# One attention bias in two made by ScalarE in the first turn, and the branch on the mask flag moved from mid-kernel to the end of the setup

## Chip, cores, metric

One NeuronCore of a Trainium2 chip runs the whole program. The metric is device time in microseconds of one execution, as the median of the runs. The kernel is written by hand, engine by engine, with semaphores: TensorE (PE, with its weight loads shown apart as PEld), VectorE (DVE), ScalarE (ACT), GpSimd (POOL), and SyncE (SP), which issues nearly all DMAs.

## What is computed

Two transformer layers over x of shape 8 x 512 x 256 with 16 heads of width 16. The first layer adds to the scores a bias that depends on the pair of positions and, by a factor, on the head:

```
# layer 0
h = layer_norm(x) * g + b, modulated by gelu(time_emb) @ Wt + bt
scores = q @ k.T / 4 - torus_dist[None] * torus_scale[head]
scores = where(pad, -1e30, scores)          # mask_BxS_bf1
x = x + softmax(scores) @ v @ Wout;  x = x + gelu(layer_norm(x) @ W1 + b1) @ W2 + b2
# layer 1: no such bias; keys masked by mask_BxS_bk0
ada = silu(c @ ada1) @ ada2 -> shifts, scales, gates of both branches
x = x + gate * modulate(norm(attention(x))); x = x + gate * modulate(norm(mlp(x)))
```

## The kernel before

The program is a setup ("prologue"), then N = 16 **turns**, then an epilogue. Turns 0 to 7 are layer 0 for the eight sequences (B = 8), turns 8 to 15 are layer 1. Each engine has its own program and its own `prologue`, `turn(n)` and `epilogue`; `run` strings them together. A turn also carries dense work of its neighbours (the table FIRST says which piece goes into which step): turn n does projections for sequence n+1 and the MLP of n-1, so turn 0 has less matmul work than turns 1 to 7, since nothing comes before it.

A turn of layer 0 has 32 **units** (a head and half of the queries each) of two 128x512 score tiles. In step k, PE does `scores(k)` (two matmuls, each into its own PSUM bank, so tile t waits until DVE has read tile t-2), every fourth step (k = 7, 11, ..., 31) `attend` (32 small matmuls), then `turn_unit(k-2)` (eight transposes), every fourth step (k = 9, 13, ...) `to_tokens`, and the dense pieces. DVE's `shift_scores(u)` (L1406) adds the bias to the scores, writes `shifted` and the row maximum; POOL's `subtract_max(u)` (L633, two instructions) follows; PE transposes the result; ACT's `exps(u)` (L1117, two instructions) takes the exponential.

The bias of a unit, 128x1024 elements, is one multiplication of `dist` by the head's `scale`. In the kernel before it is made by POOL (L626) for three units in four and by ACT (L1106) for the units with u % 4 == 3. There are two bias buffers, so that `make_bias(u)` waits for the shift of unit u-2. Both engines are in-order: POOL makes the bias of unit k+2 behind `subtract_max(k)`, and ACT makes it behind `exps(k-1)`, that is `exps(u-3)`, and ahead of `take_out` (L1125) and the dense pieces of its step k+1. DVE's wait counts the biases made so far, on one semaphore for each maker.

Layer 1 exists in two versions: a short one, for when no key is masked outside the last 128, and a general one. DVE computes a flag from the masks in its prologue (L1493 to L1499); SP stores it to DRAM (L481), in the kernel before behind the first two groups of q and k rows and the modulation rows. Before turn 8 each of the five engines waits for the store, loads the flag into a register and branches to one of two copies of turns 8 to 15. Here the short version is taken.

SP's prologue, after the loads: it stores two quarters of the q and k rows of sequence 0 (`store_half`, L373), loads the first group back in the layout that PE needs (`load_group(0, 0)`, L397 to L409), stores the other quarters, loads the second group, stores `mod_rows` and the flag, and copies rows of ones. PE's first scores wait for the first group.

DVE's prologue ends with the modulation rows (L1503 to L1510) and the low halves of `w_out` and `w_up` (L1226).

Of the kernel before, what the change touches and what calls it, by code (L numbers as in the profile page):

```python
# [18 lines left out]
def build(nc, d, out):  # L19
    B, L, D = d["x"].shape  # L20
# [15 lines left out]
    UNITS = 2 * H  # L36
# [11 lines left out]
    N = 2 * B  # L48
# [53 lines left out]
    def amid(n, k):  # L102
        return n > 0 and k in AMID

    def bias_by_act(u):
        return u % 4 == 3

    def pass_of(piece, n):
        m = n - 1 if piece[0] in BACK else n + 1 if piece[0] in FRONT else n
# [21 lines left out]
    with ExitStack() as ctx:  # L131
# [6 lines left out]
        def sem(name):  # L138
            return ctx.enter_context(nc.semaphore(name))
# [8 lines left out]
        flags = dram("flags", (1, 1), I32)  # L148
# [86 lines left out]
        early_flag = sb("early_flag", [1, 1], I32)  # L235
# [29 lines left out]
        s = {name: sem(name) for name in names}  # L265
# [51 lines left out]

        def run(eng, prologue, turn, epilogue):
            prologue()
            for n in range(B):  # L320
                turn(n)
            eng.wait_ge(s["flag_stored"], 16)
            flag = eng.value_load(flags[0:1, 0:1], min_val=0, max_val=1)
            with eng.If(flag > 0):
                chosen["any"] = 1
                for n in range(B, N):
                    turn(n)
                epilogue()
                chosen["any"] = 0
            with eng.Else():  # L330
                for n in range(B, N):
                    turn(n)
                epilogue()

# [3 lines left out]
        def _(sp):  # L338
# [106 lines left out]
            def prologue():  # L445
                with nc.allow_non_contiguous_dma(reason="small vectors laid on partitions"):
                    load_x(0)
                    load_mask(0)
                    load(cond_t[:, 0, :], d["cond_1024"][:, 0:P].rearrange("b p -> p b"), "cond_loaded")
                    load(cond_t[:, 1, :], d["cond_1024"][:, P:D].rearrange("b p -> p b"), "cond_loaded")  # L450
                    load(w_t, d["L0_cond_Wt"].rearrange("(c p) n -> p c n", p=P), "cond_loaded")
                    load(bt_col[:, :], d["L0_cond_bt"].rearrange("(c p) -> p c", p=P), "cond_loaded")
                    load(ln1_gb[:, 0, :], d["L0_cond_ln1_g"].rearrange("(c p) -> p c", p=P), "cond_loaded")
                    load(ln1_gb[:, 1, :], d["L0_cond_ln1_b"].rearrange("(c p) -> p c", p=P), "cond_loaded")
                    load(raw_qkv, d["L0_cond_Wqkv"].rearrange("(c p) n -> p c n", p=P), "wqkv_loaded")
                    load(scale[:, :], d["L0_cond_torus_scale"].unsqueeze(0).broadcast_to([P, H]), "dist_loaded")
                    load(dist[:, :, :], d["L0_cond_torus_dist"][0].rearrange("(t p) k -> p t k", p=P), "dist_loaded")
                    load(ada1, d["L1_cond_ada1_w"].rearrange("(c p) n -> p c n", p=P), "ada_loaded")
                    load(ada1_col[:, :], d["L1_cond_ada1_b"].rearrange("(c p) -> p c", p=P), "ada_loaded")
                    load(ada2, d["L1_cond_ada2_w"].rearrange("(c p) n -> p c n", p=P), "ada_loaded")  # L460
                    load(ada, d["L1_cond_ada2_b"].unsqueeze(0).broadcast_to([B, 6 * D]), "ada_loaded")
                    load(all_masks[:, :], d["mask_BxS_bk0"][:, 0:EARLY], "masks_loaded")
                    load(ln2_gb[:, 0, :], d["L0_cond_ln2_g"].rearrange("(c p) -> p c", p=P), "rest_loaded")
                    load(ln2_gb[:, 1, :], d["L0_cond_ln2_b"].rearrange("(c p) -> p c", p=P), "rest_loaded")
                    load(out_bias[:, :], d["L1_cond_proj_b"].unsqueeze(0).broadcast_to([P, D]), "rest_loaded")
                    load(raw_out[0], d["L0_cond_Wout"].rearrange("(c p) n -> p c n", p=P), "wout_loaded")
                    load(raw_up[0], d["L0_cond_W1"].rearrange("(c p) n -> p c n", p=P), "wup_loaded")
                    load_down("L0_cond_", "W2", "b1", "b2")
                x_free(0)
                load_x(1)  # L470
                store_half(0, 0)
                store_half(0, 1)
                sp.wait_ge(s["ones_set"], 2)
                load_group(0, 0)
                store_half(0, 2)
                store_half(0, 3)
                load_group(0, 1)
                sp.wait_ge(s["mod_ready"], 1)
                sp.dma_start(mod_rows, mod_out).then_inc(s["mod_stored"], 16)
                sp.wait_ge(s["flag_ready"], 1)  # L480
                sp.dma_start(flags, early_flag[:, :]).then_inc(s["flag_stored"], 16)  # L481
                for a in range(2):
                    for x in range(2):
                        at = PEAK_AT + 2 * a + x
                        sp.dma_start(k_rows[at:at + 1, :, :, a, :].bitcast(F32),
                                     q_rows[MASK_AT:KROWS, 0:2, :, :].bitcast(F32)).then_inc(s["row_ones"], 16)
# [115 lines left out]
        def _(pool):  # L602
# [127 lines left out]
            def turn(n):  # L730
                if short(n):
                    short_turn(n)
                    return
                if n < B:
                    make_bias(n, 0)
                    make_bias(n, 1)
                    if 0 < n < B - 1:
                        inverse_std(n + 1, 0)
                    for k in range(UNITS):
                        subtract_max(n, k)  # L740
                        if k + 2 < UNITS and not bias_by_act(k + 2):
                            make_bias(n, k + 2)
                        if k == 4 and n == 0:
                            inverse_std(1, 0)
                        if k == 11 and n > 0:
                            inverse_std(n - 1, 1)
                        if k in ADD_BIAS and n > 0:
                            add_bias(n - 1, ADD_BIAS[k])
                        if k == 18:
                            pool.wait_ge(s["bias_ready"], 24 * n + k + 3 - (k + 3) // 4)  # L750
                            mask(n + 1)
                    if n + 1 == B:
                        value_mask(B)
                    return
                back(n - 1)
                if n + 1 < N:
                    mask(n + 1)
                    value_mask(n + 1)
                if n > B:
                    inverse_std(n - 1, 1)  # L760
# [290 lines left out]
        def _(act):  # L1051
# [120 lines left out]
            def turn(n):  # L1172
                if short(n):
                    for p in range(HEAD_STEPS):
                        for k in range(3 * p, 3 * p + 2):
                            for piece, m in pieces(HEADS, k, n):
                                dense(piece, m)
                        if p == 0 and n - 2 >= B:
                            normalize(n - 2)
                        if 6 <= p < 6 + 2 * G and p % 2 == 0:  # L1180
                            take_heads_out(n, (p - 6) // 2)
                        if 4 <= p < 4 + H // 2:
                            for a in range(2):
                                head_exp(n, 2 * (p - 4) + a)
                        if 2 <= p < 2 + H // 2:
                            load_peaks(n, p - 2)
                        for piece, m in pieces(HEADS, 3 * p + 2, n):
                            dense(piece, m)
                        if n == B and p == 6:
                            take_high(w_out, raw_out[1], "wout_loaded", "out_high", 2)  # L1190
                        if n == B and p == HEAD_STEPS - 1:
                            take_high(w_up, raw_up[1], "wup_loaded", "up_high", 2)
                    return
                for k in range(STEPS):
                    if k >= OUT and (k - OUT) % 4 == 0:
                        take_out(n, (k - OUT) // 4)
# [1 line left out]
                        dense(piece, m)  # L1198
                    if 1 <= k <= UNITS:
                        exps(n, k - 1)  # L1200
                    if n < B and k + 2 < UNITS and bias_by_act(k + 2):
                        make_bias(n, k + 2)
                    if n == B - 1 and k in (6, 7):
                        take_qkv_high(k - 6)
# [18 lines left out]
        def _(dve):  # L1223
# [172 lines left out]
            def shift_scores(n, u):  # L1396
                for i in range(2):
                    t = 2 * u + i
                    if n < B and i == 0:
                        if bias_by_act(u):  # L1400
                            dve.wait_ge(s["act_bias_ready"], 8 * n + u // 4 + 1)
                        else:
                            dve.wait_ge(s["bias_ready"], 24 * n + u + 1 - (u + 1) // 4)
                    dve.wait_ge(s["scores_ready"], TILES * n + t + 1)
                    if n < B:
                        dve.tensor_tensor_reduce(shifted[:, u % 3, i, :], score_bank[t % 2], bias[:, u % 2, i, :],  # L1406
# [220 lines left out]
```

## Time and profile before

| | us |
|---|---|
| median of 3 runs (1373.4, 1373.43, 1377.46) | 1373.43 |
| the profiled execution's own time | 1377.58 |
| its span, first to last instruction | 1375.7 |

| engine | busy, us | share of the span |
|---|---|---|
| PE | 1287.0 | 94% |
| DVE | 796.0 | 58% |
| POOL | 754.5 | 55% |
| ACT | 744.4 | 54% |

The first scores of turn 0 start 44.42 us into the span, its last transposes run at about 125 us, and the branch lies between 855 and 860 us. The profile gives for each instruction its start and duration and, for an engine that sat idle before it, how long and what released it. Unit u of turn 0 is the u-th pair of L1406 instructions from 45.38 us on.

### The profile page before, as it was taken

The numbers are of one execution on the slowest core, as the hardware profiler recorded it, in microseconds if no ns is written. First come the engines' busy times: TensorE is split into PE (matmuls) and PEld (weight loads), VectorE is DVE, ScalarE is ACT, GpSimd is POOL, SyncE is SP. The second block draws the span as 40 slices with busy tenths as digits, with TensorE's granted clock in tenths as the row PEclk, the third lists the DMA queues.
The fourth block names the chain that finished last, engine by engine and source line by source line (L and its number), as shares of the span: only waits on it lengthen the run. The fifth ranks groups of instructions, "written<-read, shape, count | busy, mean of one in ns | idle before, by whom it ended". The sixth has DMA issues, their size and how long they took to land. (4 is left out here: it accounts for less than half of the span.)

```text
span 1375.7 us, 24533 instructions
## 1 busy us (share of the span) xinstructions
PE 1287.0 (94%) x8789; PEld 995.1 (72%) x8789; DVE 796.0 (58%) x2240; ACT 744.4 (54%) x1246; POOL 754.5 (55%) x939
## 2 busy tenths in 40 slices
PE   4799999999999999999999998899999999999878
PEld 3567778778778778778778776767677676766656
DVE  3766845845845845845844843556656566564552
ACT  3466674674674674674674673454444444444431
POOL 3688876876876876866866864101224032240323
PEclk9899999999999999999999999899999999999888
DMA  8533231331331331331331340726243352434100
GB/s 257 145 96 91 63 116 41 77 116 39 79 116 37 80 117 35 81 117 33 80 121 30 94 132 28 225 72 201 76 155 126 115 169 77 154 108 118 47 2 31
DMA packets 98259, 133.98 MB, mean 97 GB/s; under 512 B 16802, under 2 KB 51498, under 8 KB 98130
## 3 DMA queue, kind: packets, MB, share of 16 engines
q1 hardware_dynamic: 96850, 131.80, 32.5%
q8 instruction: 73, 1.20, 0.4%
q10 hardware_dynamic: 1280, 0.53, 0.2%
q14 instruction: 56, 0.46, 0.1%
HBM read 72.64 MB, written 58.75 MB: 96 GB/s over the span
## 5 line engine op out<-in xcount | busy, mean ns | idle before, releaser
L1406 DVE CUSTOM_DVE_ANT_0 shifted<-score,bias 128x512 f32<-128x512 f32 x512 | 332.1, 686 | 281.1 <-PE score L873 202.5
L633 POOL TENSOR_SCALAR shifted<-shifted,row_max 128x512 f32<-128x512 f32 x512 | 362.3, 720 | 171.3 <-DVE row_max L1406 168.4
L1117 ACT ACTIVATE probs<-turned 128x512 f32<-128x512 f32 x512 | 277.6, 595 | 218.8 <-PE turned L885 218.6
L885 PE MATMUL turned<-ident,shifted 128*128 128x128 f32 x2048 | 269.6, 274 | 4.4 <-ACT probs L1117 4.3
L885 PEld LDWEIGHTS turned<-ident,shifted 128*128 128x128 f32 x2048 | 232.8, 141 | 56.3 <-issue 32.7
L801 PE MATMUL dense<-w_down,hidden 128*128 128x256 f32 x1024 | 261.8, 382 | 2.4 <-ACT hidden L1098 2.4
L626 POOL TENSOR_SCALAR bias<-dist,scale 128x1024 f32<-128x1024 f32 x192 | 214.5, 1118 | 13.5 <-DMA down_bias<-in_L_cond_b 13.5
L873 PE MATMUL score<-k_rows,q_rows 97*128 97x512 f32 x512 | 202.2, 456 | 14.1 <-DMA k_rows<-mask_neg 5.2
L801 PEld LDWEIGHTS dense<-w_down,hidden 128*128 128x128 f32 x1024 | 178.1, 190 | 36.9 <-issue 9.6
L781 PE MATMUL dense<-feat_m,w_up 128*128 128x512 f32 x768 | 192.9, 403 | 9.4 <-DVE feat_m L1363 9.4
L781 PEld LDWEIGHTS dense<-feat_m,w_up 128*128 128x128 f32 x768 | 144.5, 193 | 42.4 <-issue 11.7
L873 PEld LDWEIGHTS score<-k_rows,q_rows 97*128 97x128 f32 x512 | 92.5, 191 | 48.3 <-DVE row_max L1406 32.4
L1098 ACT ACTIVATE hidden<-dense,up_bias 128x512 f32<-128x512 f32 x128 | 87.3, 688 | 73.9 <-PE dense L781 73.6
L900 PE MATMUL pv<-probs,v_ext 128*32 128x256 f32 x2048 | 123.8, 382 | 0.2 <-DVE attn L1431 0.2
L647 POOL CAST mask_colf<-mask_col 128x4 f32<-128x4 uint8 x8 | 1.5, 186 | 188.9 <-PE pv L952 181.2
L781 PE MATMUL dense<-feat_a,w_qkv 128*128 128x512 f32 x384 | 102.3, 410 | 2.8 <-DVE feat_a L1360 2.8
L1133 ACT ACTIVATE probs<-turned 128x512 f32<-128x512 f32 x128 | 69.4, 596 | 57.4 <-PE turned L942 57.3
L900 PEld LDWEIGHTS pv<-probs,v_ext 128*32 128x32 f32 x2048 | 60.2, 109 | 53.6 <-issue 14.3
L1440 DVE TENSOR_REDUCE row_max<-score 128x8 f32<-128x1024 f32 x64 | 78.4, 1225 | 35.1 <-PE score L923 34.0
L781 PEld LDWEIGHTS dense<-feat_a,w_qkv 128*128 128x128 f32 x384 | 70.6, 194 | 16.5 <-issue 3.2
L1085 ACT ACTIVATE qk_high<-dense 128x512 fp32r<-128x512 f32 x64 | 38.2, 598 | 74.2 <-PE dense L781 55.2
L1106 ACT ACTIVATE bias<-dist,scale 128x1024 f32<-128x1024 f32 x64 | 73.7, 1151 | 0.0
(138 smaller groups left out, 1472.0 us busy)
## 6 DMA issues: line engine op xcount, KB each, us to landing
qk_rows<-qk_high SPq DMA_DIRECT2D x128, 256.0 KB
q_rows<-qk_rows SPq DMA_DIRECT2D x64, 384.0 KB
qk_rows<-qk_low SPq DMA_DIRECT2D x64, 256.0 KB
k_rows<-qk_rows SPq DMA_DIRECT2D x68, 192.0 KB
x_in_t<-in_x SPq DMA_DIRECT2D x8, 512.0 KB, 4.8
x_res<-in_x SPq DMA_DIRECT2D x8, 512.0 KB, 5.6
x_mid<-x_norm SPq DMA_DIRECT2D x8, 512.0 KB, 3.3
x_in_t<-x_mid SPq DMA_DIRECT2D x8, 512.0 KB, 4.1
```

Of the source, the lines that this page charges most:

```text
L626: pool.tensor_scalar(bias[:, u % 2, :, :], dist[:, 2 * half:2 * half + 2, :], scale[:, h:h + 1], 0.0, ALU.mult, ALU.add).then_inc(s["bias_ ...
L633: ins = pool.tensor_scalar(shifted[:, u % 3, i, :], shifted[:, u % 3, i, :], -1.0, row_max[:, t % 6:t % 6 + 1], ALU.mult, ALU.add)
L781: mm = pe.matmul(out_ap, left, right, start=(i == 0), stop=(i == len(terms) - 1))
L801: mm = pe.matmul(bank_of(piece, m)[:, 0:D], hidden[:, c, P * i:P * i + P], w_down[:, c, :], start=(c == 0), stop=(c == FCH - 1))
L873: pe.matmul(score_bank[t % 2], q_rows[0:KROWS, g % 2, j // 2, q0:q0 + P], k_rows[0:KROWS, g % 2, j // 2, j % 2, :], start=True, stop=True) ...
L885: mm = pe.transpose(turned_bank[z % 2][:, HALF * kk + P * i:HALF * kk + P * i + P], shifted[:, u % 3, i, P * kt:P * kt + P], ident[:, :])
L900: mm = pe.matmul(pv_bank[SLOT * j:SLOT * j + SLOT, 0:HALF], v_ext[:, kt, HG * (gq // 2) + j, :], probs[:, (4 * gq + j) % RING, kt, :], sta ...
L1098: act.activation(hidden[:, i, :], bank[:, :], ACT.Gelu_apprx_tanh if m < B else ACT.Gelu, bias=up_bias[:, i:i + 1]).then_inc(used(piece, m ...
L1106: act.activation(bias[:, u % 2, :, :], dist[:, 2 * half:2 * half + 2, :], ACT.Copy, scale=scale[:, h:h + 1]).then_inc(s["act_bias_ready"], 1)
L1117: act.activation(probs[:, u % RING, 2 * pair:2 * pair + 2, :], turned_bank[z % 2][:, :].rearrange("p (a c) -> p a c", a=2), ACT.Exp)\
L1406: dve.tensor_tensor_reduce(shifted[:, u % 3, i, :], score_bank[t % 2], bias[:, u % 2, i, :], 1.0, 3.0e38, ALU.add, ALU.min, row_max[:, t % ...
L1440: dve.tensor_reduce(row_max[:, :].rearrange("p (a t) -> p t a", a=2), pair_scores, mybir.AxisListType.X, ALU.max).then_inc(s["peak_ready"], 1)
```

## The change

In turn 0 ACT makes the bias of every odd unit; the other turns keep one in four. `make_bias(0, 1)`, which POOL made ahead of the units, goes to the head of ACT's turn. The waits count biases with a function. The flag is stored ahead of the first group of rows, and all engines branch at the end of their prologue, so that all 16 turns stand in both copies.

```diff
-    def bias_by_act(u):
-        return u % 4 == 3
+    def bias_by_act(n, u):
+        return u % 2 == 1 if n == 0 else u % 4 == 3
+    def biases(n, u, act):
+        return sum(bias_by_act(m, v) == act for m in range(n + 1) for v in range(UNITS if m < n else u + 1))
...
         def run(eng, prologue, turn, epilogue):
             prologue()
-            for n in range(B):
-                turn(n)
             eng.wait_ge(s["flag_stored"], 16)
             flag = eng.value_load(flags[0:1, 0:1], min_val=0, max_val=1)
             with eng.If(flag > 0):
                 chosen["any"] = 1
-                for n in range(B, N):
+                for n in range(N):
                     turn(n)
                 epilogue()
                 chosen["any"] = 0
             with eng.Else():
-                for n in range(B, N):
+                for n in range(N):
                     turn(n)
                 epilogue()
...
                 store_half(0, 1)
+                sp.wait_ge(s["flag_ready"], 1)
+                sp.dma_start(flags, early_flag[:, :]).then_inc(s["flag_stored"], 16)
                 sp.wait_ge(s["ones_set"], 2)
                 load_group(0, 0)
...
                 sp.dma_start(mod_rows, mod_out).then_inc(s["mod_stored"], 16)
-                sp.wait_ge(s["flag_ready"], 1)
-                sp.dma_start(flags, early_flag[:, :]).then_inc(s["flag_stored"], 16)
...
                     make_bias(n, 0)
-                    make_bias(n, 1)
+                    if not bias_by_act(n, 1):
+                        make_bias(n, 1)
...
-                        if k + 2 < UNITS and not bias_by_act(k + 2):
+                        if k + 2 < UNITS and not bias_by_act(n, k + 2):
                             make_bias(n, k + 2)
...
+                if n == 0 and bias_by_act(0, 1):
+                    make_bias(0, 1)
                 for k in range(STEPS):
...
-                    if n < B and k + 2 < UNITS and bias_by_act(k + 2):
+                    if n < B and k + 2 < UNITS and bias_by_act(n, k + 2):
                         make_bias(n, k + 2)
...
-                        if bias_by_act(u):
-                            dve.wait_ge(s["act_bias_ready"], 8 * n + u // 4 + 1)
+                        if bias_by_act(n, u):
+                            dve.wait_ge(s["act_bias_ready"], biases(n, u, True))
                         else:
-                            dve.wait_ge(s["bias_ready"], 24 * n + u + 1 - (u + 1) // 4)
+                            dve.wait_ge(s["bias_ready"], biases(n, u, False))
```

## Rows read from the trace of the kernel before

**Rows 1.** The page, busy time by engine.
```profile
PE 1287.0 (94%) x8789; PEld 995.1 (72%) x8789; DVE 796.0 (58%) x2240; ACT 744.4 (54%) x1246; POOL 754.5 (55%) x939
```
**Rows 2.** Busy by window: length, PE, PEld, DVE, ACT, POOL, PEclk, DMA share, GB/s.
```profile
88.00:110.00 22.00, 21.46 (x177) 15.72 (x176) 14.74 (x51) 14.45 (x27) 21.26 (x28) 1.00 0.52 178
...
231.00:331.00 100.00, 98.89 (x782) 78.55 (x781) 59.65 (x184) 64.09 (x108) 77.63 (x97) 1.00 0.29 80
```
**Rows 3.** Waits from 44 to 128 us: total, times, longest.
```profile
DVE shifted L1406 <- ACT bias L1106: 8.5, 7, 2.0
...
DVE shifted L1406 <- POOL bias L626: 2.2, 2, 1.4
```
**Rows 4.** Timeline, units 24 to 27 of turn 0: start, duration, engine, instruction.
```profile
106.32 1.09 ACT L1117 ACTIVATE probs<-turned 128x512 f32<-128x512 f32 x2 [0.38 <-PE turned L885]
...
107.04 0.69 DVE L1406 CUSTOM_DVE_ANT_0 shifted<-score,bias 128x512 f32<-128x512 f32 x1
...
107.86 1.11 POOL L626 TENSOR_SCALAR bias<-dist,scale 128x1024 f32<-128x1024 f32 x1
...
108.35 0.71 PE L873 MATMUL score<-k_rows,q_rows 97*128 97x512 f32 x2
...
109.14 0.68 DVE L1406 CUSTOM_DVE_ANT_0 shifted<-score,bias 128x512 f32<-128x512 f32 x1
...
110.50 1.15 ACT L1106 ACTIVATE bias<-dist,scale 128x1024 f32<-128x1024 f32 x1
...
110.94 1.93 PE L900 MATMUL pv<-probs,v_ext 128*32 128x256 f32 x32
```
**Rows 5.** Timeline, exponentials of unit u-3 and shift of u, u 9 and 13.
```profile
65.45 1.09 ACT L1117 ACTIVATE probs<-turned 128x512 f32<-128x512 f32 x2 [0.94 <-PE turned L885]
...
66.61 0.69 DVE L1406 CUSTOM_DVE_ANT_0 shifted<-score,bias 128x512 f32<-128x512 f32 x1 [0.79 <-POOL bias L626]
...
75.79 1.09 ACT L1117 ACTIVATE probs<-turned 128x512 f32<-128x512 f32 x2 [0.38 <-PE turned L885]
...
77.91 0.69 DVE L1406 CUSTOM_DVE_ANT_0 shifted<-score,bias 128x512 f32<-128x512 f32 x1 [1.49 <-PE score L873]
```
**Rows 6.** Timeline, end of the setup.
```profile
31.29 1.54 SPq L373 DMA_DIRECT2D qk_rows<-qk_high  x1
...
31.77 0.14 DVE L1499 CAST early_flag<-early_any 1x1 int32<-1x1 f32 x1
...
38.84 0.36 SPq L403 DMA_DIRECT2D q_rows<-qk_rows  x1
...
39.21 0.68 DVE L1503 TENSOR_TENSOR shifted<-turned,shifted 8x512 f32<-8x512 f32 x1 [1.04 <-PE turned L985]
...
41.88 2.27 DVE L1226 TENSOR_TENSOR w_up<-probs,w_up 128x2048 fp32r<-128x2048 f32 x1
...
44.42 1.19 PE L873 MATMUL score<-k_rows,q_rows 97*128 97x512 f32 x2 [5.25 <-DMA k_rows<-mask_neg]
...
45.38 0.69 DVE L1406 CUSTOM_DVE_ANT_0 shifted<-score,bias 128x512 f32<-128x512 f32 x1 [1.23 <-PE score L873]
```
**Rows 7.** Timeline around the branch ahead of turn 8.
```profile
854.84 0.38 PE L909 MATMUL pv<-ident,head_out 128*128 128x128 f32 x2
...
859.57 0.62 SPq L409 DMA_DIRECT2D k_rows<-mask_neg  x1
859.68 1.65 PE L781 MATMUL dense<-w_qkv,feat_a 128*128 128x256 f32 x6 [4.46 <-issue]
...
865.26 0.41 SPq L438 DMA_DIRECT2D dist<-in_L_cond_proj_w  x1
...
866.54 0.42 DVE L1376 TENSOR_TENSOR x_res<-x_res,dense 128x256 f32<-128x256 f32 x1 [0.42 <-PE dense L781]
```
**Rows 8.** The load of `x_res` issued at 856.07 us, issue to landing.
```profile
DMA to landing us min/median/max: 6.6/6.6/6.6
```
**Rows 9.** Busy by window behind the branch, columns as in rows 2.
```profile
860.00:862.00 2.00, 2.00 (x11) 2.00 (x11) 0.00 (x0) 0.47 (x1) 0.00 (x0) 0.50 1.10 293
```

More of the change, by code:

```diff
@@ L749, in turn @@
                         if k == 18:
-                            pool.wait_ge(s["bias_ready"], 24 * n + k + 3 - (k + 3) // 4)
+                            pool.wait_ge(s["bias_ready"], biases(n, k + 2, False))
                             mask(n + 1)
```

## The prediction

> **What bounds the kernel now.** I read first the busy times [rows 1]: PE is busy for 94% of the span, the other engines for 54 to 58%, so an edit to ACT or POOL pays only where a stage isn't bound by PE. The windows tell the stages apart [rows 2]. In turns 1 to 7 PE is busy for 98.9 of 100 us. In turn 0, from 88 to 110 us, PE has 21.46 of 22 and POOL 21.26 of 22: both look full, and POOL is the engine that the change relieves. So the question for turn 0 is who waits for POOL. The waits of that turn answer [rows 3]: DVE waited 2.2 us in all for a bias of POOL, twice, and 8.5 us for a bias of ACT, seven times in eight units. POOL is full but in time; the bias that comes late is ACT's, and the change makes more of those.
>
> The timeline shows why [rows 4]. DVE's shift of unit 25 starts at 107.04, right behind unit 24's. PE's scores of unit 26 start at 108.35, DVE's shift of unit 26 at 109.14, ACT's bias of unit 27 runs from 110.50 to 111.65, and DVE waits for it; but in that step PE has `attend`, 1.93 us from 110.94, so the lateness of unit 27 falls under PE's own work. Units with u % 4 == 1 have no `attend` in their step. POOL's bias of unit 26 ends at 107.86 + 1.11 = 108.97, before 109.14: POOL makes it, by 0.17 us.
>
> Setup and branch are read from the timeline too. PE's first scores start at 44.42, released by the DMA of the first group, and DVE's first shift at 45.38 [rows 6]. At the branch PE's last transposes start at 854.84 and end at 855.22, and its next matmul starts at 859.68, after 4.46 us of "issue" idle [rows 7]: nothing but the flag load and the jump. SP, whose instructions are the issues themselves, shows the same price: last issue done at 859.57 + 0.62 = 860.19, next one at 865.26, so **5.07 us** [rows 7].
>
> **Part 1, the branch taken out of the middle.** PE goes straight from 855.22 to turn 8. That would give 4.46 us and more, because in 860 to 862 us the granted clock was 0.50, the lower level of 1.2 GHz, after the 4.46 us of idle [rows 9], and without the idle there is nothing to lower it. What is late next is the load of `x_res`: it lands 6.6 us after its issue at 856.07 [rows 8], at 862.67, and the first `wout` tile's addition, at 866.54 now [rows 7], can't start before 862.7. That is 3.8 us earlier for the first tile. The other `wout` matmuls run meanwhile in the other two banks, and the fourth, which needs the first bank back, then follows at once, so the stream behind comes 3.8 to 4.4 us earlier. I take 4.4, near PE's gap. The ends are 3.8, and 5.7: PE's 4.84 us from issue to issue plus half of the 1.65 us that its first six matmuls took at half the clock [rows 7].
>
> **Part 2, the branch put at the end of the setup.** SP stores the flag right after an issue that ends at 31.29 + 1.54 = 32.83, the flag is ready at 31.91, and SP's next issue waits until 38.84 anyway for the quarters to land [rows 6]: the flag's issue is hidden by that wait, at no cost. I assume it landed by 38.9, with the stores before it. Each engine then pays 5.07 us from where it arrives. ACT and POOL arrive earlier, at 38.9: free at 44.0, and one bias of 1.15 us each is done by 45.2, before DVE's 45.38. PE arrives when DVE's third `ada` addition ends, 39.21 + 0.68 = 39.89: free at 44.96, 0.5 us behind 44.42. SP does its branch before its next wait of turn 0; hidden, unless that slack is gone. DVE is the last: its subtraction for `w_up` starts at 41.88 and ends at 44.15 [rows 6]. Does the flag load wait for its start or its end? PE's row speaks for the start: from 854.84, when the transposes are issued, to 859.68 is 4.84 us, close to SP's 5.07, whereas from their end it is 4.46. I take the start: 41.88 + 5.07 = 46.95 against 45.38, **+1.6 us**; from the end it is 49.22, +3.8. At the low end nothing, if DVE's arrival falls before the flag's landing.
>
> The Trainium skill (Perfetto Trace Analysis, DVE / Act Engine Instruction) says that DVE's sequencer pushes an instruction into a wait queue and is free for the next one while it still waits for its semaphores. By that rule DVE would reach the flag before 41.88 and the sum would be 1.1 to 1.6 us lower. PE's gap doesn't look like that: an engine running ahead of its waits would have loaded the flag while it waited for the `head_out` that released the transposes at 854.84, and no gap would be seen.
>
> **Part 3, eight biases from POOL to ACT.** POOL loses 8 x 1.11 = 8.9 us, which hides behind other work: at most the 2.2 us of [rows 3] are to be had. ACT gains 8 x 1.15 = 9.2 us, each behind the exponentials of unit u-3. For unit 25 those run 106.32 to 107.41 [rows 4]; the bias ends at 108.56, and DVE shifts unit 25 at 108.6 instead of 107.04, 1.55 later. PE's scores of unit 26 need both banks of unit 25: the first is free at about 109.3, the second at 109.95, where now both matmuls run from 108.35 to 109.06. So the transposes, DVE's shift of 26 and `attend` behind them all come about 1.3 us later. PE has nothing else in that step, and the groups follow one another without slack, so this is paid in full. Units 17, 21 and 29 repeat it with 1.1 to 1.3 us. For unit 9 the exponentials end at 66.54 and the bias at 67.69, against a shift at 66.61 [rows 5]: +1.1 for DVE, of which I pass on 1.0. For unit 13 they end at 76.88, the bias at 78.03, against 77.91, with PE busy on `qk`: +0.1. Units 1 and 5 cost nothing: the first is made before the units begin, the second is hidden by the statistics that DVE does ahead of its shift. Sum 1.3 x 2 + 1.2 + 1.1 + 1.0 + 0.1 = **+6.0 us**. Ends: -2.2, if only POOL's waits went, and +9.2, if each bias of ACT were paid in full.
>
> **Sum.** -4.4 + 1.6 + 6.0 = +3.2 us. The profiled execution took 1377.58 us, of which 1375.7 are span; it becomes 1380.8. It lies 4 us over the median of 1373.43, beside the highest of the three runs; the same +3.2 on the median gives **1376.6 us**, 0.23% slower. A measurement of this kernel tells about 0.3%, 4.1 us, from no change, so that my sum stays within it.
>
> **The rivals.**
> - *DVE's branch counts from the end of its last instruction* (slower, over the bound). Place: 44.15 us, DVE. Price 3.8 instead of 1.6: sum +5.4, 1378.8 us. It decides once DVE starts its first shift later than 47.9, where the sum passes 4.1. For it: the flag is loaded with DVE's queue behind a 2.27 us instruction. Against it: PE's 4.84.
> - *POOL is the bound of turn 0* (faster). POOL is full for 21.26 of 22 us [rows 2], and bias 26 is ready with 0.17 us to spare. If the cadence follows POOL, five groups of four units without or with little dense work shrink by one bias, 1.11 each: -5.6 in place of +6.0, sum -8.4, 1365.0 us. Against it: 2.2 us of waits on POOL.
> - *ACT's bias is hidden* (within 0.3%). If PE had slack in those steps, part 3 costs 0 to 2: sum -1.8, 1371.6 us. For it: PE's rows in turn 0 show waits here and there. Against it: the chain in [rows 4].
> - *The change doesn't do what it says*: the flag lands late behind the stores, and all engines branch later. Each microsecond beyond 40.2 is paid once. I count this with the first rival.
>
> **How the numbers follow.** My own sum 0.43, first rival 0.25, POOL 0.13, hidden bias 0.19. Of my own case 0.36 lies within 0.3% and 0.07 above, as parts 1 and 3 each have ends 1 to 3 us off; of the hidden bias 0.14 lies within and 0.05 below. Together: faster 0.18, same 0.50, slower 0.32. The range leaves out the POOL case and a little at the top: 1369.0 covers the hidden bias with a larger gain at the branch, 1381.5 the first rival with part 3 at +8.7.
>
> **What would show it.** Right: the timeline has no gap of PE before turn 8; DVE's first shift at 46.5 to 47.3; waits of DVE on ACT's bias in turn 0 about twice the 8.5 us; turn 0 from first to last shift about 6 us longer. Wrong: a first shift near 49.2 (first rival); groups of turn 0 shorter than now (POOL); waits on ACT doubled, but PE's scores no later (hidden bias); `x_res` not what the first `wout` addition waits for.

## The result, and the profile after

| | before | changed |
|---|---|---|
| median of 14 runs each, us | 1374.33 (1372.57 to 1378.01) | 1380.6 (1376.82 to 1385.64) |
| ratio | | 1.0039, 95% interval 1.0029 to 1.005 |
| profiled execution / its span, us | 1377.58 / 1375.7 | 1382.92 / 1380.7 |

The change makes the kernel 0.39% slower, 5.4 us by the ratio, 5.0 us between the two profiled spans. I had forecast +3.2 us, too little to be told from no change; what came is clear of it. The lines that answer to [rows 6] and [rows 4] are these. First the timeline of the changed kernel (start, duration, engine, instruction, idle before it) around the start of turn 0:

```profile
42.65 2.27 DVE L1232 TENSOR_TENSOR w_up<-probs,w_up 128x2048 fp32r<-128x2048 f32 x1
42.87 3.06 POOL L629 TENSOR_SCALAR bias<-dist,scale 128x1024 f32<-128x1024 f32 x1 [27.55 <-issue]
...
45.54 1.22 PE L877 MATMUL score<-k_rows,q_rows 97*128 97x512 f32 x2 [5.59 <-issue]
...
49.65 0.69 DVE L1412 CUSTOM_DVE_ANT_0 shifted<-score,bias 128x512 f32<-128x512 f32 x1 [4.73 <-issue]
```

PE is at its first scores at 45.54, about where I had put it (44.96), but DVE sits idle for 4.73 us behind its last subtraction and shifts unit 0 at 49.65, not at 46.95. Next units 24 to 28 of turn 0:

```profile
112.55 0.69 DVE L1412 CUSTOM_DVE_ANT_0 shifted<-score,bias 128x512 f32<-128x512 f32 x1 [1.05 <-PE score L877]
...
113.24 1.08 ACT L1121 ACTIVATE probs<-turned 128x512 f32<-128x512 f32 x2 [0.39 <-PE turned L889]
...
114.21 1.15 ACT L1110 ACTIVATE bias<-dist,scale 128x1024 f32<-128x1024 f32 x1
...
115.39 0.69 DVE L1412 CUSTOM_DVE_ANT_0 shifted<-score,bias 128x512 f32<-128x512 f32 x1 [1.54 <-ACT bias L1110]
...
122.25 0.69 DVE L1412 CUSTOM_DVE_ANT_0 shifted<-score,bias 128x512 f32<-128x512 f32 x1 [1.04 <-PE score L877]
```

This is the step that the prediction walked through: exponentials of unit 22, ACT's bias of unit 25 behind them, and DVE waiting 1.54 us for it. From unit 24's shift to unit 25's it is 2.84 us, against 1.41 before (105.63 to 107.04). From unit 24 to unit 28 the four units take 122.25 - 112.55 = 9.70 us; before they took 8.64 (105.63 to 114.27). The waits of this turn, which answer to [rows 3]:

```profile
POOL shifted L636 <- DVE row_max L1412: 22.5, 25, 4.5
...
DVE shifted L1412 <- ACT bias L1110: 18.3, 13, 2.0
```

DVE's wait on ACT's bias went from 8.5 to 18.3 us. POOL, now relieved, waits 25 times for DVE in this turn, where it waited 9 times before. Last, the place where the branch was, which answers to [rows 7] and [rows 9]; in the second fence the columns are those of [rows 2]:

```profile
864.34 0.38 PE L913 MATMUL pv<-ident,head_out 128*128 128x128 f32 x2
864.45 0.77 PEld L785 LDWEIGHTS dense<-w_qkv,feat_a 128*128 128x128 f32 x6
864.47 0.95 PE L785 MATMUL dense<-w_qkv,feat_a 128*128 128x256 f32 x6
...
870.75 1.08 DVE L1382 TENSOR_TENSOR x_res<-x_res,dense 128x256 f32<-128x256 f32 x3 [1.40 <-DMA x_res<-in_x]
...
872.03 4.28 PE L785 MATMUL dense<-feat_a,w_qkv 128*128 128x512 f32 x18
```
```profile
866.00:868.00 2.00, 1.58 (x12) 1.13 (x11) 1.47 (x3) 1.58 (x3) 0.00 (x0) 1.00 1.06 274
```

The gap is gone, the clock stays at 1.00, and the same six matmuls take 0.95 us, not 1.65. The first `wout` addition now waits for the load of `x_res`, 1.40 us, as forecast.

Followed through the trace, the 5.0 us are made up so: first shift +4.27 us (of which 0.77 is the setup itself, whose last subtraction starts at 42.65 instead of 41.88; the profile of the bias change alone, with the branch in its old place, has it at 42.66 too); turn 0 from the first to the 33rd shift 83.70 instead of 78.93, +4.77; turns 1 to 7 +0.46; the old place of the branch, up to the `qk` matmuls (868.31 before, 872.03 now, against transposes at 854.84 and 864.34) -5.78; layer 1 +1.3.

### The profile page after: what moved, and what is told of

The parts are those of the page before. It is cut to its first block and busy times, and to the rows that moved or that the text cites. A ratio compares the mean times of both kernels' runs of the same rounds, so it can differ in the third digit from the quotient of the medians.

```text
span 1380.7 us, 24534 instructions
## 1 busy us (share of the span) xinstructions
PE 1291.0 (94%) x8789; PEld 995.9 (72%) x8789; DVE 796.1 (58%) x2240; ACT 752.2 (54%) x1254; POOL 749.1 (54%) x931
## 5 line engine op out<-in xcount | busy, mean ns | idle before, releaser
L629 POOL TENSOR_SCALAR bias<-dist,scale 128x1024 f32<-128x1024 f32 x184 | 208.3, 1133 | 27.5 <-issue 27.5
L785 PE MATMUL dense<-feat_m,w_up 128*128 128x512 f32 x768 | 193.1, 403 | 10.1 <-DVE feat_m L1369 9.4
L1446 DVE TENSOR_REDUCE row_max<-score 128x8 f32<-128x1024 f32 x64 | 78.4, 1225 | 34.9 <-PE score L927 33.8
L1110 ACT ACTIVATE bias<-dist,scale 128x1024 f32<-128x1024 f32 x72 | 82.9, 1151 | 7.3 <-issue 7.3
```

The costliest lines, as they stand in the source:

```text
L629: pool.tensor_scalar(bias[:, u % 2, :, :], dist[:, 2 * half:2 * half + 2, :], scale[:, h:h + 1], 0.0, ALU.mult, ALU.add).then_inc(s["bias_ ...
L785: mm = pe.matmul(out_ap, left, right, start=(i == 0), stop=(i == len(terms) - 1))
L1110: act.activation(bias[:, u % 2, :, :], dist[:, 2 * half:2 * half + 2, :], ACT.Copy, scale=scale[:, h:h + 1]).then_inc(s["act_bias_ready"], 1)
L1446: dve.tensor_reduce(row_max[:, :].rearrange("p (a t) -> p t a", a=2), pair_scores, mybir.AxisListType.X, ALU.max).then_inc(s["peak_ready"], 1)
```

## The experiments

All ratios are to the kernel before, timed beside each experiment on the same chip. Its own median moved between them (1374.33 us beside the changed kernel, 1377.04 beside runs 1 to 4, 1375.81 beside runs 5 to 8, 1375.31 beside runs 9 and 10), so that medians of different experiments compare only by their ratios. Runs 4, 5, 7 and 9 are single executions: they are read by their traces and not by their times.

**1. The biases alone** (branch and flag store in their old places, so the turns behind the branch are `range(B, N)` again).

```diff
             prologue()
+            for n in range(B):
+                turn(n)
             eng.wait_ge(s["flag_stored"], 16)
...
-                sp.wait_ge(s["flag_ready"], 1)
-                sp.dma_start(flags, early_flag[:, :]).then_inc(s["flag_stored"], 16)
...
                 sp.dma_start(mod_rows, mod_out).then_inc(s["mod_stored"], 16)
+                sp.wait_ge(s["flag_ready"], 1)
+                sp.dma_start(flags, early_flag[:, :]).then_inc(s["flag_stored"], 16)
```

> Part 3 alone: odd units of turn 0 by ACT, branch and flag store where they were before. Theory (ACT's bias comes late because it stands behind the exponentials): turn 0 from the first to the 33rd shift takes 4.8 us more than the 78.9 of before, as in the changed kernel (83.7), DVE's waits on ACT's bias double from 8.5 to about 18 us, time +4 to +6 us, 1379 us. Rival (the longer turn 0 comes from PE's late start and a longer stretch at the lower clock after it, that is from the branch): turn 0 stays at 79 to 80 us and the time within 1 us of before.

Measured: 1382.47 us, ratio 1.0036 (1.0022 to 1.005). The first shift is at 45.02, turn 0 takes 83.93 us, and the waits in turn 0 are those of the changed kernel:

```profile
DVE shifted L1414 <- ACT bias L1112: 18.4, 13, 2.2
```

So the bias costs about 5 us by itself, without any late start: the rival falls.

**2. The branch alone.**

```diff
-        return u % 2 == 1 if n == 0 else u % 4 == 3
+        return u % 4 == 3
```

> Parts 1 and 2 alone: flag stored early, branch at the end of the setup, biases as before. Theory: first shift about 3.5 to 4.3 us later than 45.4, the stream at the first wout additions of turn 8 gains 5.8 us against before, so -1.5 to -2.5 us net, 1372 us; turn 0 takes 79 us. Rival (the branch costs as much at the start as it gave in the middle, and the late start also drags the half clock into turn 0): 1375 us or more, turn 0 81 us or more.

Measured: 1375.75 us, ratio 0.9991 (0.9982 to 1.0). First shift 49.52, turn 0 78.38 us, `qk` matmuls behind the old branch at 866.38 instead of 868.31. The stream is 3.6 us late at the end of turn 7 and 1.93 us early at `qk`: 5.5 us gained there. Span 1373.6, 2.1 under before. Beside it the kernel before took 1377.04, so the gain is 1.3 us, a little under the 1.5 to 2.5 expected and hardly to be told from none; the 1375 us or more of the rival is met as a number, but not its turn 0 of 81 us or more. The trace has each term as the theory put it, and turn 0 is no longer than before.

**3. ACT's bias ahead of the exponentials.**

```diff
+                    ahead = n == 0 and k + 2 < UNITS and bias_by_act(n, k + 2)
+                    if ahead:
+                        make_bias(n, k + 2)
                     if 1 <= k <= UNITS:
                         exps(n, k - 1)
-                    if n < B and k + 2 < UNITS and bias_by_act(n, k + 2):
+                    if n < B and k + 2 < UNITS and bias_by_act(n, k + 2) and not ahead:
                         make_bias(n, k + 2)
```

> The whole change, but in turn 0 ACT makes the bias of unit u ahead of the exponentials of unit u-3 instead of behind them. Theory (the place in ACT's order is what costs): DVE's waits on ACT's bias fall from 18 us to under 6, turn 0 goes from 83.7 back to 79 us or a little under, time 4 to 6 us under the changed kernel, 1375 us. Rival (ACT has too much work in turn 0 wherever the bias stands, the exponentials come late instead): turn 0 stays over 82 us, with waits of PE on ACT's probs in place of DVE's.

Measured: 1378.02 us, ratio 1.0006 (0.9996 to 1.0015), against 1.0039 for the changed kernel; turn 0 79.63 us. ACT still makes 16 biases there, but DVE's waits no longer have ACT's bias among them:

```profile
DVE shifted L1415 <- PE score L877: 23.2, 15, 3.8
ACT probs L1121 <- PE turned L889: 16.8, 11, 2.4
```

It is the place in ACT's order that costs, not the amount of work. Against the changed kernel the ratio falls by 0.33%, 4.5 us, as expected (4 to 6 us). A little is left: from unit 16 on each group of four units takes 0.2 to 0.3 us more than before, where it took 1.0 to 1.1 more in the changed kernel. Turn 0 is still not shorter than the 78.4 us of run 2, where POOL makes three biases in four: relieving POOL brings nothing even when ACT's biases are in time.

**4. DVE's branch ahead of its last two subtractions.**

```diff
                 ins.then_inc(s["mod_ready"], 1)
+
+            def rest():
                 take_low(w_out, raw_out[0], "out_high", "out_split", 1)
                 take_low(w_up, raw_up[0], "up_high", "up_split", 1)
```

In both copies behind the branch, DVE calls `rest` first. The rest is the whole change, ACT's biases included.

> The whole change, but DVE loads the flag and branches ahead of its two last subtractions for w_out and w_up (0.67 and 2.27 us) instead of behind them. Theory (the flag load waits until DVE's queue is empty, then 4.7 us): both orders are the same sum, first shift at 49.7 us, give or take the 0.8 us by which two setups differ. Rival of my prediction (the load runs beside the last instruction, only slower on DVE, 7.0 us from the start of the last one): first shift 2 us later, near 51.7.

Measured, one execution: 1380.54 us, first shift at 49.53. The timeline of DVE:

```profile
40.65 0.41 DVE L1518 TENSOR_TENSOR x_res<-shifted 8x256 f32<-8x256 f32 x1
...
46.72 0.69 DVE L1234 TENSOR_TENSOR w_out<-probs,w_out 128x512 fp32r<-128x512 f32 x1 [5.66 <-issue]
47.33 2.28 DVE L1234 TENSOR_TENSOR w_up<-probs,w_up 128x2048 fp32r<-128x2048 f32 x1
49.53 0.68 DVE L1414 CUSTOM_DVE_ANT_0 shifted<-score,bias 128x512 f32<-128x512 f32 x1
```

The same first shift looks like the theory; but this setup ran 1.1 us ahead of the changed kernel's (the last `x_res` row ends at 41.06, there at 42.12), so that from there to the first shift it is 8.47 against 7.53 us. With the setup taken off, the theory wants 48.6 and the rival 50.6; 49.53 lies between them, and the question stayed open.

**5. The short subtraction last** (run 2's kernel with the two subtractions swapped).

```diff
-                take_low(w_out, raw_out[0], "out_high", "out_split", 1)
                 take_low(w_up, raw_up[0], "up_high", "up_split", 1)
+                take_low(w_out, raw_out[0], "out_high", "out_split", 1)
```

> The branch alone (second run's kernel), with DVE's two last subtractions in the other order, so that the short one (0.67 us) is the last ahead of the flag load and not the 2.27 us one. The price from the last instruction's end was 4.64 us, from its start 6.9 us. Theory (the load waits until DVE's last instruction has ended): again 4.4 to 4.8 us from the end, first shift at 49.5. Rival (a fixed price from the start of the last instruction, 6.9 us): 6.2 us from the end, first shift near 51.1. Something in between would say that part of the price runs beside the last instruction.

Measured, one execution: 1375.86 us. Only half conclusive, as another wait came in front:

```profile
44.20 0.67 DVE L1232 TENSOR_TENSOR w_out<-probs,w_out 128x512 fp32r<-128x512 f32 x1
...
47.06 1.22 PE L877 MATMUL score<-k_rows,q_rows 97*128 97x512 f32 x2 [7.16 <-DMA k_rows<-mask_neg]
...
48.64 0.69 DVE L1412 CUSTOM_DVE_ANT_0 shifted<-score,bias 128x512 f32<-128x512 f32 x1 [3.77 <-PE score L877]
```

PE's scores came at 47.06, released by the DMA of the first group, as late as in run 2 (47.05), and the profile puts DVE's wait down to them. Still, DVE's last subtraction ended at 44.87 in both runs, and the shift came 0.9 us earlier here: DVE was free of the branch within 3.77 us of its last end, less than any fixed price from the end (4.35 to 4.73 in the other runs with the change's order) and less than the 6.2 of the rival.

**6. The branch in the gaps.** The flag is computed between the first two `qk` pieces and stored behind the first quarter; DVE branches ahead of its `ada` additions, PE ahead of its wait for them; both call `rest` first in either copy. Biases as before.

```diff
                 store_half(0, 0)
-                store_half(0, 1)
                 sp.wait_ge(s["flag_ready"], 1)
                 sp.dma_start(flags, early_flag[:, :]).then_inc(s["flag_stored"], 16)
+                store_half(0, 1)
...
+            def rest():
                 for c in range(3):
                     dve.wait_ge(s["ada_ready"], c + 1)
```

> The branch alone, but each engine takes it where it would idle: the flag is computed and stored earlier (between the first two qk pieces and behind the first quarter), DVE branches ahead of its ada additions, in the gap in which it waits for PE, and PE ahead of its wait for them. Biases as before. Theory (only DVE's 3.5 us at the end of the setup kept the moved branch from paying): first shift at 45.4 to 46.5 instead of 49.5, turn 0 about 79 us, time 3 to 4 us under the run with the branch alone and 4 to 6 us under the kernel before, 1371 us. Rival (the flag lands late wherever it is stored, or the ada chain and not DVE's own order sets the start): first shift over 48 us and no gain over the branch alone.

Measured: 1371.47 us, ratio 0.9975 (0.9962 to 0.9988), span 1369.5. It beats both kernels and has the lowest ratio of this study, level with run 10's. The kernel before took 1375.81 beside it, so the gain is 3.4 us by the ratio (4 to 6 expected). First shift at 46.73, just beyond the 46.5 expected, turn 0 78.16 us. The rival's fear shows in part:

```profile
40.61 1.28 DVE L1519 TENSOR_TENSOR shifted<-score,shifted 8x512 f32<-8x512 f32 x2 [9.38 <-issue]
```

DVE idles 9.38 us there, well over a branch, because it also waits for the flag's landing: POOL, idle since 15.6 us, starts its first bias at 40.51 too. The additions that could have started at about 35.6 start at 40.61, and that costs the remaining 1.3 us of the start.

**7. Only the units that I held to be covered** (branch in its old place).

```diff
+        return u % 4 == 3 or n == 0 and u in (1, 5, 13)
```

> Branch as before; in turn 0 ACT makes, besides the units with u % 4 == 3, only those of units 1, 5 and 13, which by my walk lie under other work. Theory: turn 0 takes 78.9 to 79.3 us, as before, against 83.9 with all odd units; what costs is units 9, 17, 21, 25 and 29. Rival (each bias on ACT costs its share, about 0.6 us for each of eight): 80.8 us.

Measured, one execution: 1374.74 us, turn 0 79.17 us. As the theory has it: units 1, 5 and 13 together cost 0.24 us (units 4 to 7 take 0.51 more, units 8 to 11 0.26 less), and so the rest of the 4.8 us must lie in units 9, 17, 21, 25 and 29.

**8. Every odd unit in all turns of layer 0.**

```diff
+        return u % 2 == 1 and (n == 0 or u > 1)
```

> Branch as before; ACT makes the bias of every odd unit in all eight turns of layer 0 (unit 1 only in turn 0). Theory (where PE is the bound, dense work in the step covers ACT's bias): turn 0 longer by 5 us as in the first run, turns 1 to 7 by less than 0.5 us each, time within 4 us of the first run. Rival (the late bias costs in every turn, the dense pieces don't cover it): 3 to 5 us more in each of turns 1 to 7, 1400 us or more.

Measured: 1398.9 us, ratio 1.017 (1.0147 to 1.0192). Both expectations miss, mine by more. POOL's mask step stands at unit 18 of every turn, so its starts give the turns; here those of turns 0, 1, 2 and 7, of the first run's kernel and then of this one:

```profile
95.33 0.61 POOL L645 TENSOR_SCALAR mask_neg<-mask_row 1x512 fp32r<-1x512 uint8 x1
184.63 0.61 POOL L645 TENSOR_SCALAR mask_neg<-mask_row 1x512 fp32r<-1x512 uint8 x1
288.15 0.61 POOL L645 TENSOR_SCALAR mask_neg<-mask_row 1x512 fp32r<-1x512 uint8 x1
...
807.04 0.61 POOL L645 TENSOR_SCALAR mask_neg<-mask_row 1x512 fp32r<-1x512 uint8 x1
```
```profile
94.44 0.61 POOL L645 TENSOR_SCALAR mask_neg<-mask_row 1x512 fp32r<-1x512 uint8 x1
184.18 0.61 POOL L645 TENSOR_SCALAR mask_neg<-mask_row 1x512 fp32r<-1x512 uint8 x1
291.92 0.61 POOL L645 TENSOR_SCALAR mask_neg<-mask_row 1x512 fp32r<-1x512 uint8 x1
...
822.07 0.61 POOL L645 TENSOR_SCALAR mask_neg<-mask_row 1x512 fp32r<-1x512 uint8 x1
```

From turn 1 to turn 2 it is 107.74 us against 103.52, and from turn 2 to turn 7 530.15 against 518.89, that is 11.26 over five turns: 4.2 us once, then 2.3 us a turn. From 292 to 800 us DVE waits 83.2 us for ACT's bias, 52 times, against 45.7 us, 20 times, in the first run's kernel, and PE is busy for 496.50 of these 508 us against 502.43. So even where PE is busy 98.9 of 100 us, a bias that is late for DVE makes PE late, since PE's next scores wait for the banks that DVE reads. A full engine is no cover by itself. That only work placed in that very step covers is my reading; no run moved such work, and the 4.2 us of the first of these turns are not explained.

**9. A longer queue on DVE** (run 2's kernel with two more subtractions of 2.2 us).

```diff
+                dve.wait_ge(s["up_high"], 1)
+                for i in range(2):
+                    dve.tensor_tensor(hidden[:, 4 * i:4 * i + 4, :].rearrange("p (c a) n -> p c (a n)", c=DC), raw_up[0],
+                                      w_up[:, 0, :, :].bitcast(F32), ALU.subtract)
                 take_low(w_up, raw_up[0], "up_high", "up_split", 1)
```

> The branch alone, with two more subtractions of 2.27 us each put on DVE between the one for w_out and the one for w_up; their results go to a part of hidden that is overwritten before it is read, and change nothing. Theory (the flag load starts only when DVE's queue is empty): the gap behind the last subtraction stays at 4.3 to 4.8 us and the first shift moves by the whole 4.5, to 54.0. Rival (the load starts when the last instruction has been handed over, and in the kernel with the branch alone 6.9 us ran from there, partly beside it): part of the price is hidden beside the longer queue, the gap shrinks to 0 to 2 us and the first shift lies between 49.5 and 51.5.

Measured, one execution: 1375.61 us.

```profile
42.29 9.06 POOL L629 TENSOR_SCALAR bias<-dist,scale 128x1024 f32<-128x1024 f32 x2 [26.68 <-issue]
...
42.58 4.47 DVE L1521 TENSOR_TENSOR hidden<-probs,w_up 128x2048 f32<-128x2048 f32 x2
...
46.98 2.27 DVE L1232 TENSOR_TENSOR w_up<-probs,w_up 128x2048 fp32r<-128x2048 f32 x1
...
50.28 0.69 DVE L1412 CUSTOM_DVE_ANT_0 shifted<-score,bias 128x512 f32<-128x512 f32 x1 [1.03 <-POOL bias L629]
```

4.4 us more of queued work moved the first shift by 0.76 us only, from 49.52 to 50.28. The gap shrank from 4.64 to 1.03 us, and what ended it was POOL's bias, so the branch may have been done still earlier. The theory that I had taken up after the result, that the load waits for an empty queue, falls; the load and the jump run beside work that DVE has already been given.

**10. The flag stored by ACT** (run 6's kernel, the store on ACT's queue behind its second `qk` piece).

```diff
+                    if piece == ("qk", 1):
+                        act.wait_ge(s["flag_ready"], 1)
+                        act.dma_start(flags, early_flag[:, :]).then_inc(s["flag_stored"], 16)
```

> As the run with the branch in the gap, but ACT issues the flag's store behind its second qk piece, on its own DMA queue, so that it does not stand behind SP's stores of the rows. Theory (in that run the flag landed late, DVE sat 9.4 us of which about half was waiting for the landing, and the first shift came at 46.7): DVE starts its ada additions at 36 to 38 us instead of 40.6, first shift at 45.4 to 45.7, time about 1 us under that run, 1370.5 us. Rival (the landing is set by the DMA engines' load, not by the queue it is issued on): ada additions at 40 us again, no gain.

Measured: 1372.31 us, ratio 0.9978 (0.9968 to 0.9987), the same as run 6 within the intervals. DVE's additions start at 38.51 (36 to 38 expected), the first shift at 46.92 (45.4 to 45.7 expected).

```profile
27.28 0.49 ACTq L1171 DMA_DIRECT2D flags<-early_flag  x1
...
37.92 2.22 POOL L629 TENSOR_SCALAR bias<-dist,scale 128x1024 f32<-128x1024 f32 x2 [22.54 <-issue]
...
38.51 1.28 DVE L1520 TENSOR_TENSOR shifted<-score,shifted 8x512 f32<-8x512 f32 x2 [7.12 <-PE score L991]
...
45.96 1.19 PE L877 MATMUL score<-k_rows,q_rows 97*128 97x512 f32 x2 [6.28 <-DMA k_rows<-mask_neg]
```

DVE came 2.1 us earlier than in run 6, as the store was issued 2.7 us earlier. From the end of the issue to POOL's first bias it took 10.1 us (27.77 to 37.92), as on SP's queue in run 6 (30.43 to 40.51): the other queue brought nothing. And no gain was left to take, because PE's first scores waited until 45.96 for the DMA of the first group. That load now sets the start.

## Why the prediction was right or wrong

The direction and the place of each term were right, and the time lies in the range, which reached to 1381.5, by 0.9 us. The forecast itself, no change that can be told, was not the outcome: the 0.39% belong to the slowdown to which I had given 0.32. The sum was 2.2 us short by the ratio. That it came so near is in part luck: three terms were off by 1.2, 1.4 and 1.9 us, which cancel to 0.7, and half of the measured 5.0 us lies outside of them. By its steps:

- **The biases (part 3): mechanism right, size 1.2 us too high.** +6.0 forecast, +4.8 in the trace, and the bias change alone measures 0.36%, about 5 us. By groups of four units, from unit 8 on, the trace has +0.76, -0.02, +1.09, +0.96, +1.06 and +1.06, and the first eight units -0.14; the walk had 1.0 and 0.1 for units 9 and 13, 1.3 for unit 25, and 1.1 to 1.3, 3.6 together, for units 17, 21 and 29. Run 2, which starts as late, but with the old biases, has the first group 0.65 us shorter as well; against it turn 0 is 5.3 us longer. The delay of DVE came out nearly exact (1.55 forecast, 1.43 from unit 24's shift to unit 25's), but not all of it reached the next group. Run 3 shows the cause, run 7 the units. POOL as the bound of turn 0 is refuted by run 3, where it is relieved, ACT is in time, and no group shrinks by the 1.11 us of that rival.
- **The branch taken out (part 1): mechanism right, size 1.4 us too low.** -4.4 forecast, -5.8 in the changed kernel and -5.5 in run 2. The load of `x_res` was late next, as said, but it landed 5.2 us after its issue and not 6.6, which is the 1.4 us. I had taken a duration from one DMA of one execution as if it were fixed; the upper end, 5.7, held nearly.
- **The branch put in (part 2): the step that failed.** +1.6 forecast; DVE's first shift came 3.5 us later than the setup alone explains. The other engines came back as forecast or earlier (PE 45.54 for 44.96, with the setup 0.8 late; ACT 42.53 and POOL 42.87 for 44.0). For DVE I had counted SP's 5.07 us from the start of its last subtraction. From there to the first shift it took 7.0 us (42.65 to 49.65). The choice "start, not end" was right in kind: run 9 shows the load running beside queued work. The price was wrong: 5.07 is what SP paid at 860 us, and DVE at 43 us paid up to 7.0. The first rival gave +3.8 for this term and hit the time, but for a reason that run 9 refutes.
- Taken together the terms give 3.5 + 4.8 - 5.8 = +2.5, and the rest to 5.0 is the setup's 0.8, turns 1 to 7 with 0.5 and layer 1 with 1.3. The setup's 0.8 is in most of the profiles of these experiments too, so it lies between executions and not in the change. The other two aren't explained. The two parts run alone add up to +0.36% and -0.09%, 0.27%, against 0.39% together, which the intervals allow.

The Trainium skill's rule (Perfetto Trace Analysis, DVE / Act Engine Instruction), that DVE's sequencer hands an instruction on and is free, bore on this term. Run 9 agrees so far as execution goes: 6.7 us of queued subtractions covered all but 1.03 us of the gap. That it also runs ahead of unfulfilled waits, which would have made the start free, no run here shows.

Why DVE's price is 5.7 us in run 4, at most 3.8 from the last end in run 5 and 7.0 from the last start in the changed kernel, stays open; I didn't separate the flag's read from the fetch of the code behind the jump. Two things in the traces bear on it. The profile counts seven DMA packets of instruction queues from 40 to 48 us in the changed kernel (q8 two, q14 five), and none from 35 to 51 us in the kernel before, so code is fetched there; it doesn't say for which engine. And ahead of the flag's wait DVE's program also waits for its own modulation rows: counted from the end of the last of them (42.07 to 42.12 us) the first shift comes 7.53 us later in the changed kernel, 7.45 in run 2, at most 6.6 in run 5 and at most 8.2 in run 9. A price of 6.6 to 7.5 us that starts there, whatever is queued behind, fits these four as well, and no run here tells it from one that starts at a subtraction.

## What to carry to other kernels

Before moving work to an idle engine, ask what it would stand behind in that engine's order and when its reader needs it: eight biases of 1.15 us cost 4.8 us behind the exponentials and about 1 us ahead of them (turn 0 79.63 us, against 78.93 and 78.38 with the old biases), and the engine that was relieved had kept DVE waiting for only 2.2 us. Moving a runtime branch doesn't remove its price, here some 4 to 7 us on PE, SP and DVE; put each engine's branch where that engine waits for something else anyway, and look then for what becomes late next.

## What was unexpected of the hardware

- A flag stored to DRAM and read back costs 7.5 to 10.1 us from the end of the store's issue to the first instruction behind the branch, the branch included (POOL, which idles for it: 9.8 in the changed kernel, 7.5 in run 4, 8.0 in run 5, 10.1 in runs 6 and 10), on SP's queue as on ACT's.
- POOL's bias, 1.12 us as a rule, took 3.06 us beside DVE's subtraction for `w_up` (first fence above), and two of them 9.06 us in run 9, of which the first, beside the three long subtractions, took 7.96 and the second 1.11. In run 4, where DVE is idle at 41.83, the same bias takes 1.12. The Trainium skill (SBUF — State Buffer, SBUF: two separate sides) tells of a port pair that DVE and GpSimd share under an exclusive lock. These rows agree: in the changed kernel DVE's subtraction ends at 44.92 and POOL's bias 1.01 us later, so that here it was POOL that stood still until DVE was done.
- The clock stayed at its upper level over the old place of the branch once PE's idle 4.46 us were gone, and the same six matmuls went from 1.65 to 0.95 us. From their start to the start of the `w_out` matmuls it is 4.25 us (864.47 to 868.72), against 5.81 before (859.68 to 865.49), so the removal gave more than the gap itself; how much of that is the clock and how much the other engines' own branches isn't separated.
